# An expert's output is added to the tokens behind the first half pair's scans, no longer ahead of them

## What is computed

```python
# layer 0, experts: every expert is computed for every token, two of eight weights are not zero
logits = xf @ w_router
topk_w, topk_idx = jax.lax.top_k(jax.nn.softmax(logits, axis=-1), TOP_K)
weights = jnp.sum(topk_w[..., None] * mask, axis=1)
h = jax.nn.gelu(jnp.einsum('te,ieh->tih', xf, w1) + b1)      # hidden 512
out = jnp.einsum('tih,ihe->tie', h, w2) + b2
out = jnp.sum(out * weights[..., None], axis=1)
# layer 1, scan over the tokens
def step(h, inp):
    dt_t, xv_t, B_t, C_t = inp
    dA = jnp.exp(dt_t[:, :, None] * A[None])
    h = dA * h + (dt_t * xv_t)[:, :, None] * B_t[:, None, :]
    y_t = jnp.einsum('bdn,bn->bd', h, C_t)
    return (h, y_t)
```

## Time and profile before

| | |
|---|---|
| median of 3 runs | 705.69 us |
| profiled execution, its own time | 706.18 us |
| span of its instructions | 704.2 us |
| granted TensorE clock, mean of the span | 0.909 |
| busy: PE, PEld, DVE, ACT, POOL | 74%, 51%, 61%, 53%, 50% |
| experts alone and attention | start to about 295 us |
| pairs 0 to 20, experts and scan | about 295 to 579 us |
| pairs 21 to 31 and the end | about 579 us to the end |

### The profile page before, as it was taken

One profiled execution on the slowest core, in us unless ns is written; L12 is line 12 of the kernel. 1 busy time (PEld: TensorE's weight loads), 2 busy tenths in 40 slices (PEclk: granted clock), 3 DMA queues, 4 the chain that ended last, 5 costly groups with the idle time before them and its releaser, 6 DMA issues. The chain is left out here.

```text
span 704.2 us, 6938 instructions
## 1 busy us (share of the span) xinstructions
PE 518.1 (74%) x2368; PEld 355.7 (51%) x2368; DVE 429.5 (61%) x727; ACT 374.5 (53%) x515; POOL 354.4 (50%) x224
## 2 busy tenths in 40 slices
PE   4587767666887888978768876876968658756773
PEld 4354545333676775666645555654646433333222
DVE  5569778526142231268944559592568588589972
ACT  1334132234645447697786786577877635543301
POOL 3138686607100102048875557596476647446661
PEclk9989898879899999999998989897999989968897
DMA  8400000000000003001101010111000021101100
GB/s 323 162 1 0 0 2 0 1 0 0 1 1 1 0 1 122 0 31 46 45 33 46 24 51 32 31 45 61 31 32 31 29 74 61 61 31 60 45 1 15
DMA packets 12564, 26.94 MB, mean 38 GB/s; under 512 B 1969, under 2 KB 7473, under 8 KB 12273
## 3 DMA queue, kind: packets, MB, share of 16 engines
q1 hardware_dynamic: 11952, 25.57, 10.3%
q10 hardware_dynamic: 576, 0.92, 0.4%
HBM read 25.31 MB, written 1.18 MB: 38 GB/s over the span
## 5 line engine op out<-in xcount | busy, mean ns | idle before, releaser
L1189 PEld LDWEIGHTS pO<-w_e,gel 128*128 128x128 f32 x1024 | 133.8, 202 | 21.3 <-issue 16.7
L931 ACT ACTIVATE gel<-pH,b_e 128x512 f32<-128x512 f32 x128 | 86.5, 686 | 94.6 <-PE pH L1179 94.0
L1189 PE MATMUL pO<-w_e,gel 128*128 128x128 f32 x1024 | 136.4, 286 | 0.0
L731 DVE TENSOR_TENSOR_SCAN Hs<-dA,HL,pCT 128x512 f32<-128x512 f32 x96 | 117.7, 1267 | 15.9 <-ACT dA L943 8.8
L702 DVE SCALAR_TENSOR_TENSOR X<-pO,wts,X 128x128 f32<-128x128 f32 x128 | 36.0, 344 | 145.0 <-PE pO L1189 145.0
L364 POOL TENSOR_TENSOR Zev<-Hs,Crow 128x1024 f32<-128x1024 f32 x32 | 77.4, 2420 | 92.7 <-DVE Hs L731 84.8
L943 ACT ACTIVATE dA<-dt,a_neg 128x512 f32<-128x512 f32 x128 | 81.8, 710 | 29.0 <-DVE Hs L731 28.7
L720 DVE TENSOR_TENSOR pCT<-u,pB 128x1024 f32<-128x1024 f32 x64 | 78.2, 1222 | 12.0 <-PE pB L1244 11.4
L1177 PE MATMUL pH<-h2h,w_e1h 128*128 128x512 f32 x128 | 64.7, 505 | 20.2 <-ACT gel L931 11.7
L1244 PE MATMUL pB<-ST,sel 96*128 96x512 bf16 x64 | 26.4, 413 | 54.7 <-DVE pCT L720 54.4
L425 POOL TENSOR_TENSOR ZA<-Qsb,S 128x1024 f32<-128x1024 f32 x16 | 37.9, 2370 | 36.2 <-DVE S L626 33.2
(11 more groups left out here) (196 smaller groups left out, 949.2 us busy)
## 6 DMA issues: line engine op xcount, KB each, us to landing
Crow<-c_rows SPq DMA_DIRECT2D x32, 512.0 KB, 3.5
w_e<-in_w_e SPq DMA_DIRECT2D x2, 2048.0 KB, 10.7
X<-in_x SPq DMA_DIRECT2D x4, 256.0 KB, 6.8
out<-h2T SPq DMA_DIRECT2D x4, 256.0 KB, 4.4
S<-in_w_mod ACTq DMA_DIRECT2D x2, 384.0 KB, 4.8
w_cx<-in_conv_row SPq DMA_DIRECT2D x1, 512.0 KB, 9.5
w_f<-in_w_f SPq DMA_DIRECT2D x2, 128.0 KB, 5.6
b_e<-in_b_e SPq DMA_DIRECT2D x1, 256.0 KB, 13.2
```

What stands on the lines that cost most here:

```text
L731: vec.tensor_tensor_scan(Hs[:, 2 * o + d, 0:w], dA[:, 4 * (p % 2) + 2 * o + d, 0:w], pU[:, d, 0:w], HL[:, d, n:n + 1] if c else 0.0, ALU.m ...
L931: nc.scalar.activation(gel[:, n % NG, 0:w], pH[n % 2][:, 0:w], ACT.Gelu_apprx_tanh, bias=b_e1[:, NK * e + k:NK * e + k + 1]).then_inc(s["m ...
L1189: ins = mm(pO[:, j * P:(j + 1) * P], gel[:, n % NG, j * P:(j + 1) * P], w_e2[:, NK * (g % E) + k, :], start=(k == 0 and j == 0), stop=(k = ...
```

## The change

In half pair (p, 0) with p from 0 to 20, VectorE's four instructions of `moe_acc` move from between the product with B and the two scans to behind the two scans and the reduce that keeps the last column. For p below 0, where there is no scan, nothing moves. No instruction is added or removed.

```diff
-                if o == 0 and 0 <= p + AHEAD - 2 < NL * E:
-                    moe_acc(p + AHEAD - 2)
+                acc = o == 0 and 0 <= p + AHEAD - 2 < NL * E
                 if p < 0:
+                    if acc:
+                        moe_acc(p + AHEAD - 2)
                     return
                 vec.wait_ge(s["mam_ub"], m + 1)
                 vec.wait_ge(s["mam_dA"], ND * (m + 1))
...
                 if c + 1 < NL:
                     vec.tensor_reduce(HL[:, :, n], Hs[:, 2 * o:2 * o + 2, w - 1:w], AX.X, ALU.max)
+                if acc:
+                    moe_acc(p + AHEAD - 2)
```

## The result

The changed kernel takes 724.61 us (median of 4 runs, 722.59 to 725.69) against 706.47 us for the kernel before in the same series. The ratio is 1.0245, with a 95% interval of 1.0200 to 1.0291: 2.4% slower. The forecast was slower, 710.8 us, in a range up to 715. The direction was right, the size was off by more than three times.

The account below looks back on a forecast made before the run. The prediction took chains of waits, not one engine, as the bound. Terms 5.0 - 1.3 + 2.5 - 1.4 + 3.5 - 1.35 - 1.8 = +5.15 us, added to 705.69, gave 710.8 us; range 703 to 715.

Parts of the forecast that it names:

- the ring: Pairs 1 to 4 and 12: ScalarE and TensorE waits set a 10.10 us pace; moves cost nothing, delays carry on.
- C: Pairs 8 to 10: late scans delay TensorE, mostly won back, then pair 10 loses again; +2.5 us.
- C': Pairs 16 to 18: same loss as in pairs 8 to 10, but old pairs were quicker; +3.5 us.
- A: Pair 0: down projection waits for accumulation behind late scans, then runs at low clock; +5.0 us.
- the clock falls at other places than these: Sign of being wrong: TensorE's low clock appears elsewhere than behind the waits in pairs 0, 8 and 16; no size.
- the low clock in all: Upper case: half clock charged fully in pairs 0, 8 to 10 and 16 to 18; sum +6.95 us.
- the 0.5 us margin: Pairs 1 to 4 and 12: accumulation behind scans still ends about 0.5 us before the down projection needs it.
- the margin isn't there: Rival, chance 0.12: some nine delay-carrying pairs each lose about 0.5 us more; 715.3 us.
- term B: Pairs 7, 15 and 19: TensorE's wait for VectorE's product goes; -1.3, -1.4 and -1.35 us.
- term E: Pair 20: scans go ahead during the down projection, shortening TensorE's wait for the product; -1.8 us.
- TensorE's own stream: Rival, chance 0.16: TensorE's own work, not its waits with ScalarE, carries the time; +0.5 us, 706.2 us.
- The relief is all that counts: Rival, chance 0.12: TensorE makes up the delayed accumulation elsewhere; 699.0 us, or 702.4 with losses in pairs 10 and 18.

Follow-up runs that it names:

- the ten pairs moved: Kernel before, with the accumulation behind the scans only in pairs 1 to 6 and 11 to 14: 713.71 us, ratio 1.0078.
- the version with six moves: Kernel before, with the accumulation behind the scans only in pairs 7, 9, 15, 17, 19 and 20: 698.36 us, ratio 0.9851.
- the filled kernel: Changed kernel plus extra matmuls during TensorE's waits in pairs 0, 8, 10, 16 and 18: 711.24 us, ratio 1.0034 to the kernel before.

## Why the prediction was wrong

**The step that failed is where the low clock was charged: only behind the waits of pairs 0, 8 and 16 (in 8 and 16 by half), nothing behind the new waits of pairs 10 and 18, and nothing in the ring, "these pairs cost and gain nothing".** In the changed kernel's trace C and C' came to 5.3 and 6.3 us in place of 2.5 and 3.5. The ring, put at nothing, came to 1.4 in pair 1 and 1.7 in pairs 11 to 14. The sum was missed by 11.25 us: 5.6 are C and C', 3.1 the ring, 1.2 the last stretch, 1.05 the start before pair 0, and the rest is mostly A. The prediction named as a sign of being wrong that "the clock falls at other places than these", and so it did.

At full clock the forecast's sum was +1.6 us; the run with TensorE kept busy, which comes near that state, is 0.34% or 2.4 us slower than before. Everything above it came back when TensorE had no long idle time before D in five pairs: some 15 us of 17 by the ratios, 12.0 of 15.4 in the traces behind pair 0's start. That the filling works through the clock, and not through another way, is shown by the shorter matmuls and by the terms, which fall near their values at full clock.

Point by point:

- *Pair 0, term A*: right, 5.35 against 5.0, the low clock included. The accumulation waits behind the scans, these for the decays, D for both.
- *C and C'*: the mechanism was right, the size was not: 5.3 and 6.3 against 2.5 and 3.5. The queue's part measured 1.7 and 2.9, against 1.5 and 2.6. The forecast gave the low clock to pairs 8 and 16, partly, and none to pairs 10 and 18. There TensorE idled 2.21 us, and D to G took 5.1 and 5.0 us, where the kernel before has 3.48 in both. Even "the low clock in all", 3.4 and 4.4, had left it out.
- *The ring*: the 0.5 us margin was worked out from the decays alone. In pair 1 VectorE is still behind with pair 0's late scans; with the ten pairs moved D(1) comes 0.44 us late for it, and the ring has no slack. The larger part is that a shift of half a microsecond changes which of TensorE's pieces run at 0.50. The rival "the margin isn't there" named this place, at 4.5 us; in the changed kernel the ring added 1.4 in pair 1 and the pairs 11 to 14 another 1.7. In the changed kernel itself D(1) did not wait for the accumulation; there the late pair 0 set the clock, as the run with only pair 0 moved shows with the same 1.4. The low clock in pair 12 also came in versions that moved none of pairs 11 to 14.
- *Pairs 7, 15, 19, term B, and pair 20, term E*: right within 0.35 us, -1.4, -1.6, -1.0 and -1.9. The relief of R(9) and R(17) was real too; in the version with six moves R(9) is 4.94 us early, but 3.0 us are lost again by G(14).
- *The rivals*: TensorE's own stream against the ring with ScalarE is decided for the ring by the filled kernel: R(0) is 2.46 us late there and G(0) 3.40, and D(1) to G(5) are all 3.40 late. "The relief is all that counts" is wrong, since the late D(0) moved G(0) by 5.35. Its 10.1 us of gain come only if the five pairs and the ten of the ring are left out, 10.6 us by the ratio and 8.1 in the trace.
- *The range* ran to 715, with about half of the lost margin in it; the bound of the forecast itself was 712.6. That bound charged the low clock only where the kernel before had shown it, beside its three waits, and not behind every new wait.

The clock's rule that the forecast weighed (the Trainium skill, page "TensorE: Matmul & The Clock Gate", section "Why this matters for your kernels": long idle gaps between bursts bring the clock back down) warned rightly. Going by it alone the prediction had +6.95 us, nearer than my +5.15, but still under half of the 16.4. This trace agrees, with 6.39 and 6.50 us of idle time and 3.78 us for what takes 1.95, and the low clock was found behind shorter gaps as well, 2.21 us in pair 10.

The last stretch, from pair 21 on, added 1.2 us through the low clock as well. From R(26) to R(27) it takes 1.66 us more than before: the granted clock is 0.50 from 655.4 to 662.2 us there, and was 0.50 only from 640.7 to 644.1 at the same place before. What stays open: what put the clock there, the 1.05 us before pair 0, and what brings the low clock into pair 12.

## What to carry to other kernels

An instruction on which another engine waits should not stand behind one that waits for a third engine, nor behind other work where its own engine is late (pairs 10 and 18). Look at each place where it moves, not at the sum of the waits: six of the 21 places made this kernel 1.5% faster, all 21 made it 2.4% slower. And where TensorE is in the ring that sets the pace, price a new idle time before it twice, once as a wait and once as half clock on what follows.

## What was not expected of the hardware

The length of the idle time alone did not tell whether the clock falls. In the kernel before, TensorE waits 2.99 us for the gelu in pair 4 and the first matmul behind it is at full speed:

```profile
345.18 0.51 PE L1177 MATMUL pH<-h2h,w_e1h 128*128 128x512 f32 x1 [2.99 <-ACT gel L931]
```

With pair 1 moved and nothing else, the same wait in the same pair has the same length, and the matmul takes 0.79 us:

```profile
347.95 0.79 PE L1181 MATMUL pH<-h2h,w_e1h 128*128 128x512 f32 x1 [2.99 <-ACT gel L935]
```

Over the last 14 us before that matmul, TensorE's rows in the two traces have the same lengths and distances to within 0.03 us. What differs is the time at which they come, 2.3 us later when both are counted from the `row_b` of pair 0's first state, and what lies further back, the half clock in pair 2. It was no chance of one run: in four kernels that share the late D(1), with 16, 18, ten and one pairs moved, G is 2.33 to 2.35 us late in pair 2 and 3.75 in pair 4 (3.87 with 18).
